# Latent attention with a routed feed-forward layer on one core: queries projected with their dims in partitions, two tiles at a time, rope rows placed through DRAM, slots taken group by group, and a new order at the end

## The reference

```python
q = layernorm(x); q_c = q @ W_dq                       # 96 latent dims
q_nope, q_rope = (q_c @ W_uq), (q_c @ W_qr)            # 16 heads of 128 and of 64
kv_c = ctx @ W_kvc                                     # 64 latent dims
k_nope, v, k_rope = kv_c @ W_uk, kv_c @ W_uv, kv_c @ W_kr
scores = (q_nope . k_nope + rope(q_rope) . rope(k_rope)) / sqrt(192)
attn = softmax(where(id - 8 <= key <= id, scores, -1e30))
x = x + concat_heads(attn @ v) @ W_o
n = layernorm(x)
top2 = top_k(n @ gate_w + gate_b, 2)                   # of 8 experts
x = x + mean over top2 of relu(n @ expert_w[e] + expert_b[e])
```

## Time and profile before

| | us |
|---|---|
| median of 3 runs (391.34 to 395.19) | 392.6 |
| the profiled execution | 392.47 |
| its span, first to last instruction | 390.6 |
| PE busy, PEld busy | 353.8, 290.2 |
| DVE, ACT, POOL busy | 276.5, 262.5, 234.0 |
| mean granted clock of TensorE | 0.979 |

### The profile page before, as it was taken

The page is one execution under the profiler, slowest core; times in us unless marked ns, Lnnn a source line. Parts: engine busy times, 40 slices in busy tenths (PEclk is TensorE's granted clock), DMA queues, the critical chain, the costliest instruction groups (busy, mean ns, idle before and its releaser), DMA issues.

```text
span 390.6 us, 10358 instructions
## 1 busy us (share of the span) xinstructions
PE 353.8 (91%) x2507; PEld 290.2 (74%) x2507; DVE 276.5 (71%) x1395; ACT 262.5 (67%) x907; POOL 234.0 (60%) x326
## 2 busy tenths in 40 slices
PE   0979999999999999999999999999999788999940
PEld 0866777776778887888888888888887677888730
DVE  2358789687887878778777777778779566444365
ACT  1327777788877887877878877878788544555430
POOL 4626456367987767768577675776865355455500
PEclk9989999999999999999999999999999999999985
DMA  8955040000000000000000000000000354453178
GB/s 273 345 198 215 3 110 3 1 3 27 2 30 1 30 10 17 27 0 27 0 27 27 0 27 0 27 27 0 30 2 28 97 166 127 146 141 113 34 262 294
DMA packets 15094, 28.27 MB, mean 72 GB/s; under 512 B 2892, under 2 KB 10719, under 8 KB 14416
## 3 DMA queue, kind: packets, MB, share of 16 engines
q1 hardware_dynamic: 11408, 20.25, 16.3%
q0 software_dynamic: 2960, 6.94, 5.0%
q10 hardware_dynamic: 688, 0.64, 0.6%
HBM read 17.81 MB, written 10.91 MB: 74 GB/s over the span
## 4 chain that ended last, share of the span: by engine, by line
PE 73%; DVE 9%; issue 7%; POOL 5%; DMA 2%; ACT 2%; ACTq 0%; DVEq 0%; POOLq 0%
PE psum L1135 12%; PE psum L674 9%; PE psum L675 9%; PE psum L676 9%; PE psum L1205 8%; PE psum L1092 8%; PE psum L1119 6%; DVE x_all L1557 2%; DMA wcat<-in_w_kvc 2%; PE psum L1182 2%; PE psum L371 2%; POOL prob L1363 2%; PE psum L1014 1%; POOL q_sb L1349 1%; PE psum L1026 1%
## 5 line engine op out<-in xcount | busy, mean ns | idle before, releaser
L1230 ACT ACTIVATE prob<-nsc,nmax 128x128 f32<-128x128 f32 x256 | 100.7, 396 | 42.9 <-DVE nmax L1625 42.8
L1349 POOL TENSOR_TENSOR q_sb<-rope_a,rope_b 128x256 f32<-128x256 f32 x64 | 47.6, 743 | 57.6 <-DVE rope_b L1588 53.5
L1625 DVE CUSTOM_DVE_ANT_0 nsc<-psum,mask 128x128 f32<-128x128 f32 x256 | 58.9, 286 | 21.3 <-PE psum L1135 21.3
L1363 POOL TENSOR_TENSOR prob<-prob,prec 128x512 f32<-128x512 f32 x64 | 67.1, 1049 | 7.3 <-DVE prec L1596 7.3
L1135 PE MATMUL psum<-kT_all,qT 128*128 (+1 forms) x512 | 69.0, 278 | 1.1 <-ACT qT L1273 1.1
L1135 PEld LDWEIGHTS psum<-kT_all,qT 128*128 128x128 f32 x512 | 62.9, 193 | 2.4 <-ACT qT L1273 2.0
L1417 POOL DMA_INDIRECT halves<-jout,jidx x33 | 32.2, 977 | 30.2 <-ACT jout L1245 13.4
L1230 ACT ACTIVATION_READ_ACCUMULATOR prob<-nsc,nmax 128x1 f32 x256 | 48.4, 189 | 0.0
L1092 PE MATMUL psum<-ident,q_sb 128*128 128x128 f32 x256 | 42.4, 289 | 1.8 <-POOL q_sb L1349 1.7
L1092 PEld LDWEIGHTS psum<-ident,q_sb 128*128 128x128 f32 x256 | 27.2, 142 | 20.9 <-issue 12.3
L1205 PE MATMUL psum<-pT,v_cur 128*64 128x256 f32 x256 | 41.7, 405 | 0.0
(11 more groups left out here) (204 smaller groups left out, 864.7 us busy)
## 6 DMA issues: line engine op xcount, KB each, us to landing
wanted<-slots SPq DMA_DIRECT2D x33, 129.0 KB, 2.4
wo_raw<-in_w_o SPq DMA_DIRECT2D x2, 1024.0 KB, 15.5
we_raw<-in_expert_w SPq DMA_DIRECT2D x1, 2048.0 KB, 9.0
half<-halves SPq DMA_DIRECT2D x4, 512.0 KB, 7.3
x_all<-in_x SPq DMA_DIRECT2D x2, 640.0 KB, 17.9
slots<-pad_row SPq DMA_DIRECT2D x8, 129.0 KB, 3.4
we_raw<-in_ctx_near SPq DMA_DIRECT2D x1, 1024.0 KB, 12.0
out<-x_all SPq DMA_DIRECT2D x2, 512.0 KB, 4.7
```

Source lines behind the costliest of these rows:

```text
L1230: e = act.activation(prob[r][:, h, :], nsc[r][:, h, :], ACT.Exp, bias=nmax[r][:, h:h + 1], scale=-1.0, accum_out=psum_h[r][:, h:h + 1])
L1349: pool.tensor_tensor(q_sb[1 - r][:, :, KVC:P], rope_a[1 - r][:], rope_b[1 - r][:], ALU.add).then_inc(m["rope_joined"], 1)
L1363: pool.tensor_tensor(p[:], p[:], prec[1 - r][:, :].unsqueeze(2).to_broadcast([P, HG, P]), ALU.mult).then_inc(m["prob_normed"], 1)
L1625: e = dve.tensor_tensor_reduce(nsc[r][:, h, :], B_S[r][:, h, :], mask[(k // GPT) % 2][:], -SCALE, BIG, ALU.add, ALU.min, nmax[r][:, h:h + 1])
```

## The change

A slot is still one group of one tile, but the order is batch by batch, group by group, and the two tiles of the batch in turn: slot k of a batch is group k//2 of tile k%2. The two slots of one group are a **pair** (`QUADS` in the code): the even slot is tile 0, the odd one tile 1.

- Queries come out of TensorE with their dims in partitions, for the 256 rows of both tiles at once: weights are the stationary operand, the latent rows the moving one. Rope dims of a pair go to one PSUM bank in an odd slot, nope dims to another in an even slot, six matmuls of 256 columns each.
- The four transposes per slot and the copy of the turned queries are gone. ScalarE copies nope dims from PSUM to `qT` (two copies of 64x512 per pair). VectorE makes two rope products of 128x512 per pair, in the even slot, behind `oT_lo` and ahead of the reciprocal; GpSimd adds them (128x512) ahead of the probabilities; SP writes the sum to DRAM and reads it back in two DMAs into the rope rows of `qT`, a pair of slots ahead of use.
- TensorE's order in a slot: probabilities of slot i-2 turned, scores of slot i, query part, output product of slot i-3, value product of slot i-2 (in slot 3 of a batch the query part follows the output product).
- Both tiles' output products share one bank, cleared by a one-row matmul at the start of a batch; the residual sum and statistics are made for both tiles in the batch's third slot after its end.
- The end: dense pieces 0 to 3 come in slots 65 and 66, ahead of all jobs; jobs then run without dense pieces between them, with the rows and gates of tiles 14 and 15 between jobs 1 to 8; dense pieces 4 to 11 come after the last job, and the sums of `halves` between them.
- At the start the walk begins a slot earlier; the load of the expert weights and the padding of the regions move into SP's slots 0, 6 and 10.

```diff
 # TensorE
-                    for h in range(HG):
-                        mm = pe.transpose(B_QT[:, P * h:P * h + P], q_sb[r][:, h, :], ident[:])
-                    mm.then_inc(m["qT_done"], 1)
-                    mm3(pe, B_Q[:, :], qc_hi[j1][:], qc_lo[j1][:], wq_hi[:, hs, :]..., wq_lo[:, hs, :]...
+            def q_part(z, g, first):
+                for q in range(2):
+                    cols = q_cols(first + q)
+                    mm = mm3(pe, z[:, L * q:L * q + L], wq_hi[:, g, cols], wq_lo[:, g, cols], qc_hi[:], qc_lo[:])
+            def query(b, k):
+                if k % TPB and live(p + 3, QUADS):
...
+                    at_least(pe, "rope_parts", p + 3)
+                    q_part(B_R, g, 2).then_inc(m["qr_done"], 1)
+                if k % TPB == 0 and live(p + 2, QUADS):
+                    at_least(pe, "nope_copied", 2 * p + 4)
+                    q_part(B_N, g, 0).then_inc(m["qn_done"], 1)
+                    if (k - 3) % SLOTS == 0:
+                        pe.matmul(B_Y[:, :], zero16[:], ones16[0:1, :]..., start=True, stop=False)
 # VectorE
-                    dve.tensor_tensor(rope_a[1 - r][:], a, cos, ALU.mult)
-                    dve.tensor_tensor(rope_b[1 - r][:]..., sin, ALU.mult).then_inc(m["rope_parts"], 1)
+                if t == 0 and live(p + 2, QUADS):
+                    at_least(dve, "qr_done", p + 3)
+                    at_least(dve, f"qr_out{into}", ...)
+                    at_least(dve, "rope_joined", p + 2)
+                    dve.tensor_tensor(rope_c[into][:], a, ropeT[:, 0:1, :].to_broadcast([P, 2, L]), ALU.mult)
+                    dve.tensor_tensor(rope_s[:], a[:, ::-1, :], ropeT[:, 1:3, :], ALU.mult).then_inc(m["rope_parts"], 1)
+                if kn == 2 and live(nb - 1, B):
+                    batch_sum(nb - 1)
 # GpSimd
-                    pool.tensor_tensor(q_sb[1 - r][:, :, KVC:P], rope_a[1 - r][:], rope_b[1 - r][:], ALU.add)
+                if k % TPB == 0 and live(pn, QUADS):
+                    at_least(pool, "rope_parts", pn + 1)
+                    pool.tensor_tensor(into[:], into[:], rope_s[:], ALU.add).then_inc(m["rope_joined"], 1)
 # ScalarE
-                    act.copy(qT[r][:], B_QT[:, :]...)
-                    act.copy(q_sb[1 - r][:, :, 0:KVC], B_Q[:, :]...[:, :, 0:KVC])
+                act.copy(qT[into][0:KVC, odd::2, :], B_N[KVC * odd:KVC * odd + KVC, :]...)
 # SyncE
+                if k % TPB == 0 and live(pn, QUADS):
+                    at_least(sp, "rope_joined", pn + 1)
+                    sp.dma_start(rows, rope_c[into][:]).then_inc(m[f"qr_out{into}"], 16)
+                    at_least(sp, f"qr_out{into}", ...)
+                    at_least(sp, "s_done", 2 * pn - 2)
+                    for a in range(2):
+                        sp.dma_start(qT[into][KVC + QR * a:KVC + QR * a + QR, :, :],
+                                     rows[:, a, :].rearrange("(h r) n -> r h n", r=QR)).then_inc(m[f"qr_put{into}"], 16)
 # the end
-        DENSE_AFTER_JOB = {8: 0, 11: 1, 14: 2, 17: 3, 20: 4, 23: 5, 26: 6, 29: 7}
+        ROWS_AFTER_JOB = {1: NS + 1, 5: NS + 2}
+        GATE_AFTER_JOB = {3: NS + 1, 7: NS + 2}
+        CHOICE_AFTER_JOB = {4: NS + 1, 8: NS + 2}
```

More of the change, by code:

```diff
@@ L1726, in _ @@
             with sp.If(near == 1):
[L1727 to L1730 removed]
+                walk(sp, slot)
                 sp.wait_ge(S("padded"), 16 * NE)
```

706 lines of the change are left out of this document (368 added, 338 removed).

## The result

The changed kernel takes 397.80 us (median of four runs, 397.48 to 398.70) where the kernel before takes 393.36 beside it (391.34 to 395.19): a ratio of 1.0118 with a 95% interval of 1.0062 to 1.0174. I had forecast 391.0, a little faster. The time lies in the range I gave; the direction is wrong, and the interval leaves no room for it.

A forecast was written before the change was run, and what follows sets the result against it. TensorE's stream was taken to bound the slots before the change, and GpSimd's normalisation chain the pairs after it. The terms +4 - 7 + 8 - 6.5 = -1.5 against 392.47 gave 391.0 us, range 373 to 404.

The forecast's parts named there:

- the size of the end: After the last scores: jobs at GpSimd's 1.27 us per send, end at about 82 us; -6.5 us, bounds -11 and 0.
- The start: To the scores of slot 2: rope rows through DRAM and later constants delay the first score pass; +4 us, bounds +1 and +7.
- Slots 2 to 17: TensorE's saving of 0.48 us per slot comes through over 15 slots; -7 us, bounds 0 and -12.
- The 46 slots: Slots 17 to 63: a VectorE and GpSimd chain makes a pair 7.99 us, a batch 34.3; +8 us, bounds -11 and +16.
- The DMA: Rival on the rope rows' trip through DRAM: above 6.4 us per DMA the scores wait, some +69 us; chance 0.04.
- The extras vanish: Rival in the 46 slots: sends and batch sums fit into even slots' slack, 31.96 per batch, 377 us; chance 0.28.
- The longer GpSimd chain: Rival in the even slots: the chain to the normalisation takes longer; with 0.45 us more per pair, 401 us; chance 0.21.
- TensorE's pace: Rival in the 46 slots: TensorE still sets the pace, 29.3 us per batch, -21, so 362 us; chance 0.07.
- the two slower rivals: The longer GpSimd chain, near 401 us, chance 0.21, and the DMA rival, chance 0.04.

The follow-up runs named there:

- e3: Changed kernel with rows, gates and choices of the last two tiles moved from behind jobs 1 to 8 to behind jobs 9 to 18: 396.40 us, ratio 1.0106.
- e8: Changed kernel with GpSimd's constants moved to slot 0, between the second mask and the layer norm's power: 396.43 us, ratio 1.0094.
- e13: The kernel before, unchanged, profiled once more: 391.68 us, first matmul at 9.00 us.
- e15: Changed kernel with its rope table loaded by two DMAs with runs of 512 bytes in place of one with 3 KB: 397.08 us, ratio 1.0113.
- e14: Changed kernel with the four subtractions for the output weights' low parts moved from GpSimd to VectorE, in slots 13 to 15: 400.24 us, ratio 1.0179.
- e6: Changed kernel with GpSimd's rope sum moved from the even slots to behind the normalisation of the odd slots: 389.48 us, ratio 0.9917.
- e1: Changed kernel with GpSimd's rope sum behind the normalisation in even slots instead of ahead of it: 397.00 us, ratio 1.0112.
- e2: Changed kernel with GpSimd's rope sum made twice in the 20 pairs of the middle five batches: 427.86 us, ratio 1.092.
- e9: On top of e7, VectorE's copy of a tile's choice replaced by an add with one operand in PSUM: 387.05 us, ratio 0.9844.
- e7: On top of e6, the second of a tile's two sends moved behind the odd slot's normalisation, ahead of the rope sum: 388.24 us, ratio 0.9873.

## Why the prediction was wrong

**The step that failed is the size of the end**, "the jobs run at GpSimd's pace ... the last send starts at 19 + 1.7 + 32 x 1.27 = 61.3", and with it -6.5. The first job's product did come at 18.6 after the last scores (19). The first send came at 21.6, 0.9 later than I counted; the 32 intervals took 43.44 in place of 40.6; from the last send to the end were 21.1 in place of 20.7. Together that is about 4 of the forecast's error of 7.0, and alone it turns -1.5 into +2.5. The middle term is the large one: the rows, gates and choices of the last two tiles, which the change sets behind jobs 1 to 8, fall where no finished job is in stock. I put them at nothing and counted GpSimd's pace as if the first jobs were there already. e3 moves those steps back and wins 2.0 of it. In the diff the dictionaries of rows, gates and choices were in plain sight.

**The start**, +4 forecast and +6.2 measured. The constants ahead of the first mask were foreseen, and e8 puts 2.0 us on them. Not foreseen was the very first load, 2.1 us late: the table's DMA with runs of 512 bytes became one with 3 KB, and the load on ScalarE's queue got less of the DMA engines. e13 and e15 show that, and by e15 the load is worth 1.8 us at the scores of slot 2; neither it nor the constants show in the time alone. The first score pass, forecast near 32, came at 34.86, and it waited for the mask behind the constants (4.44 us in VectorE's timeline), not for the rope rows. Their trip took less than the "some 7 us": from the write's issue at 24.32 to the scores at 29.75 are 5.4. e15 shows that behind the inputs in SP's queue it holds TensorE's first scores at 29.4 by itself.

**Slots 2 to 17**, -7 forecast and -4.7 measured. Slots 2 to 9 gave 2.8 of the 3.4 that 7 x 0.48 promise; slots 9 to 17 gave 1.9 of 3.8. In the changed kernel's chain of waits TensorE's lines lead up to slot 9; from there ScalarE's exponentials and weight copies and VectorE's score passes take over, and from slot 14 GpSimd's subtractions and normalisations. e14 moved the subtractions and lost, so what exactly sets slots 9 to 17 stays open.

**The 46 slots**, +8 forecast and +6.5 measured: the chain was right, the closeness of the number is partly luck. Pairs by the starts of the odd slots' turnings: 8.24 us (209.37 to 217.61) without an extra, 8.43 with the sends of slot 4, 8.81 with those of slot 0, 9.07 with the batch sum. The extras are 0.19, 0.57 and 0.83, together 1.6 where I had 2.3, and the pair is 8.24 where I had 7.99; the two errors nearly cancel, 34.55 against 34.3. The five batches from slot 17 to 57 cost 8.3 us; the last six slots, which have no later queries to make, give 1.8 back, and I had not counted that. Wrong was TensorE's own work: without waits I had 6.84 us per pair, but it is busy for 30.65 per batch, 7.66 per pair, and in e6 a pair without a wait takes 7.66. So only 3.9 us per batch were to be won from its waits, and the pair of 6.9 that I expected of e1 was out of reach. e2 shows that the sum lies on the path, e6 that moving it turns the sign.

**The rivals.** The DMA: out, as told. "The extras vanish": no, 1.6 us remain. The longer GpSimd chain: it is longer by 0.25 us per pair, not by 0.45. TensorE's pace: no, it waits 3.9 of 34.55 us, and its own 30.65 is more than the rival's 29.3; e9, with sum, sends and copy out of the way, comes to 33.0 and still waits.

**The chances.** I gave slower by over 1% a chance of 0.26, most of it for the two slower rivals; it came by neither, but by three terms erring the same way. Two of the three were gains read from an engine's pace (TensorE's in slots 2 to 17, GpSimd's at the end) as if it set in at once and held throughout.

## What to carry to other kernels

When a chain is cut, count what stands next in the queue of each engine on it: once the sum was out of the way, the sends, a copy and the rope products each held the batch at 33.0 to 33.3 us, and of four repairs only the first gave more than 2 us. A steady pace of the last engine holds only from the moment there is work in stock, and as long as the engine ahead of it keeps up: work put in among the first jobs cost 2.0 us that e3 saved among the later ones, and dense pieces between the jobs made TensorE the slower one and cost 5. An in-order queue makes any early wait everybody's: the reciprocal ahead was worse by 11 us although VectorE had idle time.

## What the runs showed of the hardware

- A small copy on VectorE from SBUF to SBUF stood still beside GpSimd's 128x512 passes (normalisation and rope sum): 128x8 took 0.171 us in the kernel before, 0.678 (median) in the changed one, 1.740 with the sum in the odd slots and 1.732 with the sends split, each slow one ending 0.04 us behind such a pass; the same result with one operand from PSUM took 0.166 at the same place. Beside a mask pass of GpSimd (`m_after`, at 132.37 in the kernel before and 99.71 in the changed one) and beside a send alone (e7, 298.25) the copy took 0.17 all the same. By the Trainium skill, "SBUF — State Buffer", section "SBUF: two separate sides", VectorE (in a mode with two ports, or with two SBUF inputs) and GpSimd share a port pair that is locked for a whole instruction, and the loser blocks; the traces agree for the 128x512 passes, and not for the mask pass and the lone send. A copy of eight columns on the path can be dear where GpSimd is busy.
- How soon a load on one DMA queue lands hangs on the length of the runs on another: with a table in runs of 3 KB on SP's queue, a 64 KB load on ScalarE's queue lands after 9.4 us, with runs of 512 bytes after 7.0. The Trainium skill says in "DMA: Bandwidth & Descriptors", section "Queues, rings and completion order", that an engine takes turns between queues packet by packet; what was moved in the first 12 us agrees with that. ScalarE's queue in the changed kernel, then in e15 (packets, MB, share):

```profile
q10 hardware_dynamic: 570, 0.30, 8.7%
```

```profile
q10 hardware_dynamic: 688, 0.64, 23.1%
```
